# An fp32 two-stage linear layer on TensorE: the sums of x blocks and of the folded weight move from VectorE to GpSimd

## What is computed

```
cond = einsum('bsi,oi->bso', x, weight) + bias                       # 2048 x 2048
     + scale[b] * einsum('bsr,bor->bso', einsum('bsi,bri->bsr', x, a_sel), b_sel)   # rank 16
w    = (NF4[codes].reshape(-1, 64) * absmax[:, None]).reshape(2048, 2048)
out  = x + einsum('bsd,od->bso', cond, w) + bias2
```

## Time and profile before

| what | us |
|---|---|
| median of 3 runs | 2275.09 (2272.87 to 2276.41) |
| the profiled execution | 2272.21 |
| its span | 2270.1 |
| PE busy | 2189.5 (96%) |
| DVE busy | 1862.0 (82%) |
| ACT busy | 1114.2 (49%) |
| POOL busy | 0.2 |

### The profile page before, as it was taken

One profiled execution on the slowest core, in us unless ns is written; L12 is line 12 of the kernel. 1 busy time (PEld: TensorE's weight loads), 2 busy tenths in 40 slices (PEclk: granted clock), 3 DMA queues, 4 the chain that ended last, 5 costly groups with the idle time before them and its releaser, 6 DMA issues.

```text
span 2270.1 us, 32172 instructions
## 1 busy us (share of the span) xinstructions
PE 2189.5 (96%) x12194; PEld 1870.2 (82%) x12194; DVE 1862.0 (82%) x2795; ACT 1114.2 (49%) x1494; POOL 0.2 (0%) x4
## 2 busy tenths in 40 slices
PE   3589999999999999999999999999999999999999
PEld 2468877887888777889999988888988888988888
DVE  8989988987898565488887789888798888898887
ACT  7766666664666333344444444334444343443432
POOL 0000000000000000000000000000000000000000
PEclk8699999999999999999999999999999999999999
DMA  8477877887787798877777877777887777977775
GB/s 191 139 235 241 253 238 240 253 263 233 248 256 252 251 300 274 259 241 236 245 237 234 278 263 252 239 243 250 281 273 240 242 244 248 302 254 239 242 249 172
DMA packets 403535, 558.02 MB, mean 246 GB/s; under 512 B 42008, under 2 KB 256664, under 8 KB 403256
## 3 DMA queue, kind: packets, MB, share of 16 engines
q1 hardware_dynamic: 403384, 555.98, 77.4%
HBM read 427.96 MB, written 128.99 MB: 245 GB/s over the span
## 4 chain that ended last, share of the span: by engine, by line
PE 93%; DVE 5%; ACT 1%; DMA 1%; issue 0%; DVEq 0%; SPq 0%; ACTq 0%
PE ps L1332 26%; PE ps L1171 14%; PE ps L1173 14%; PE ps L1172 14%; PE ps L1333 13%; PE ps L1336 4%; PE ps L1182 2%; PE ps L1335 2%; PE ps L1215 1%; PE ps L1166 1%; DVE wq_nat L839 0%; DVE wq_nat L842 0%; DVE deq_e L858 0%; DVE deq_e L855 0%; DVE wq_nat L864 0%
## 5 line engine op out<-in xcount | busy, mean ns | idle before, releaser
L1332 PE MATMUL ps<-comb,xs 128*128 128x512 f32 x2527 | 903.3, 395 | 0.8 <-DVE comb L936 0.8
L679 ACT CAST xs<-xr 128x1024 fp32r<-128x1024 f32 x427 | 448.2, 1051 | 625.5 <-DMA xr<-xc_d 625.2
L1333 PE MATMUL ps<-comb,xs 128*128 128x256 f32 x2527 | 707.8, 280 | 0.0
L942 DVE TENSOR_TENSOR xs<-xr,xs 128x1024 fp32r<-128x1024 f32 x427 | 521.3, 1221 | 128.8 <-ACT xs L679 126.1
L1332 PEld LDWEIGHTS ps<-comb,xs 128*128 128x128 f32 x2527 | 474.3, 188 | 103.4 <-DVE comb L936 1.1
L1333 PEld LDWEIGHTS ps<-comb,xs 128*128 128x128 f32 x2527 | 475.4, 188 | 14.5
L1171 PE MATMUL ps<-wq,tile 128*128 128x512 f32 x1088 | 468.8, 431 | 0.0
L1173 PE MATMUL ps<-wq,tile 128*128 128x512 f32 x1088 | 427.9, 393 | 0.0
L1172 PE MATMUL ps<-wq,tile 128*128 128x512 f32 x1088 | 427.1, 393 | 0.0
L1171 PEld LDWEIGHTS ps<-wq,tile 128*128 128x128 f32 x1088 | 205.7, 189 | 66.0 <-issue 2.8
L1173 PEld LDWEIGHTS ps<-wq,tile 128*128 128x128 f32 x1088 | 205.6, 189 | 45.3
(11 more groups left out here) (115 smaller groups left out, 2401.0 us busy)
## 6 DMA issues: line engine op xcount, KB each, us to landing
xr<-xc_d SPq DMA_DIRECT2D x427, 512.0 KB, 3.9
raw<-in_L_cond_weight_dram SPq DMA_DIRECT2D x128, 512.0 KB, 4.3
xc_d<-rq SPq DMA_DIRECT2D x26, 1792.0 KB, 7.3
x_nat<-in_x_dram SPq DMA_DIRECT2D x128, 256.0 KB, 3.8
res<-in_x_dram SPq DMA_DIRECT2D x64, 512.0 KB, 5.3
out_dram<-res SPq DMA_DIRECT2D x128, 256.0 KB, 4.4
wc_d<-cs SPq DMA_DIRECT2D x32, 896.0 KB, 4.6
comb_raw<-wc_d SPq DMA_DIRECT2D x28, 1024.0 KB, 7.8
```

What stands on the lines that cost most here:

```text
L679: nc.scalar.copy(xs[f][:, HI, :, :], xr[f][:, LO, :, :]).then_inc(s_xhi, 1)
L942: tt(xs[f][:, LO, :, :], xr[f][:, LO, :, :], xs[f][:, HI, :, :].bitcast(F32), ALU.subtract).then_inc(s_xlo, 1)
L1332: nc.tensor.matmul(bank[:, :], x_hi, both, start=(k == 0), stop=False)
L1333: nc.tensor.matmul(bank[:, 0:HW], x_lo, high, start=False, stop=False)
```

## The change

`weight_sums` and `x_sum` are taken out of DVE's program and put, with the same operands, semaphores and waits, into a new program on GpSimd that runs over the same jobs: in job g first `weight_sums`, then `x_sum` step 3 in odd jobs, and steps 0 to 2 in even ones. ACT's and SP's programs and their waits are as before.

```diff
@@ DVE
-            def weight_sums(j, k):
...
-            def x_sum(m, step):
...
             for g in range(JOBS):
...
-                if s % 2 and s >= 3:
-                    weight_sums(j, (s - 3) // 2)
-                if s == 0 and j:
-                    weight_sums(j - 1, HK - 1)
                 if n is not None:
                     dequantise_a(n)
-                if g % 2 and 3 <= g <= 2 * UNITS + 1:
-                    x_sum((g - 3) // 2, 3)
                 if n is not None:
                     dequantise_b(n)
-                if g % 2 == 0 and 2 <= g <= 2 * UNITS:
-                    x_sum(m, 0)
...
-                if g % 2 == 0 and 2 <= g <= 2 * UNITS:
-                    x_sum(m, 1)
-                    x_sum(m, 2)
...
-            weight_sums(NS - 1, HK - 1)
@@ GpSimd
+        @block.gpsimd
+        def _(pool):
+            tt = nc.gpsimd.tensor_tensor
+
+            def weight_sums(j, k):
+                g, t0 = S1 * j + 2 * k + 2, 4 * (HK * j + k)
+                pool.wait_ge(s_evac, evacs(g))
+                if k == 0:
+                    pool.wait_ge(s_gst, 16 * (j + 1))
+                    pool.wait_ge(s_btst, 16 * min(j + 1, NS - 1))
+                b11, b21, t2, t1, b12, b22, t4n = (cs[:, f, :] for f in range(NF))
+                tt(t1, b12, b11, ALU.subtract).then_inc(s_tcomb, 1)
+                tt(b12, b22, b12, ALU.subtract).then_inc(s_tcomb, 1)
+                pool.wait_ge(s_tcomb, t0 + 1)
+                tt(t2, b22, t1, ALU.subtract).then_inc(s_tcomb, 1)
+                pool.wait_ge(s_tcomb, t0 + 3)
+                tt(t4n, b21, t2, ALU.subtract).then_inc(s_tcomb, 1)
+
+            def x_sum(m, step):
...
+            for g in range(JOBS):
+                j, s = divmod(g, S1)
+                if s % 2 and s >= 3:
+                    weight_sums(j, (s - 3) // 2)
+                if s == 0 and j:
+                    weight_sums(j - 1, HK - 1)
+                if g % 2 and 3 <= g <= 2 * UNITS + 1:
+                    x_sum((g - 3) // 2, 3)
+                if g % 2 == 0 and 2 <= g <= 2 * UNITS:
+                    for step in range(3):
+                        x_sum((g - 2) // 2, step)
+            weight_sums(NS - 1, HK - 1)
```

More of the change, by code:

```diff
@@ L1080, in _ @@
                 j, s = divmod(g, S1)
-                n, m = pieces_of(g), (g - 2) // 2
+                n = pieces_of(g)
                 if s == 1:
@@ L1157, in _ @@
             add_lora(2 * ALL_PAIRS - 1, PRODUCTS - 1)
+        @block.gpsimd
[15 more added lines that the diff above has]
+            def x_sum(m, step):
+                a11, a12, s2, s1, a21, s4, a22 = (rq[:, f, :, :] for f in range(NF))
+                if m < EARLY:
+                    pool.wait_ge(s_back, 32 * (m + 1))
+                if step == 0:
+                    pool.wait_ge(s_xcp, 4 * m + 2)
+                    ins = tt(s1, a21, a22, ALU.add)
+                elif step == 1:
+                    pool.wait_ge(s_xcp, 4 * m + 3)
+                    ins = tt(a21, a11, a21, ALU.subtract)
+                elif step == 2:
+                    pool.wait_ge(s_sums, 4 * m + 1)
+                    ins = tt(s2, s1, a11, ALU.subtract)
+                else:
+                    pool.wait_ge(s_xcp, 4 * m + 4)
+                    pool.wait_ge(s_sums, 4 * m + 3)
+                    ins = tt(s4, a12, s2, ALU.subtract)
+                ins.then_inc(s_sums, 1)
+            for g in range(JOBS):
[10 more added lines that the diff above has]
+            weight_sums(NS - 1, HK - 1)
         @block.tensor
```

## The result

The changed kernel took 2289.86 us in the median of 4 runs (2288.18 to 2291.45); the kernel before, run beside it, 2274.26 us in 4 runs (2272.87 to 2276.41). The ratio is 1.007, with a 95% interval of 1.0058 to 1.0082: **15.6 us slower**, within the range and with the sign of the forecast, which had said 23 us. Three executions among all that follow, one of E8 and two of the kernel before beside it, ran far slower (3136 to 10897 us) and are left out of every figure.

The account below looks back on a forecast made before the run. PE bounds the kernel, with DVE hidden behind it. DVE held up by GpSimd adds costs +16 us in the first slice and +6 in the next two, together +23 (rounded up): 2298 us, own range 2280 to 2320, overall 2272 to 2335.

Parts of the forecast that it names:

- its relief: DVE's lighter load: saves PE's wait of about 0.13 us at first-slice job edges, 1 us, taken as nothing.
- GpSimd's price: Eight adds a pair on GpSimd: 1.14 us for 128x512 and 0.60 for 128x256, 6.9 us a pair.
- a DVE instruction with two SBUF operands stands still: Such DVE instructions wait while a two-SBUF-operand GpSimd add runs: 5.9 us blocked a pair.
- the others: L836, L845 and L877 on DVE, taken as not held up by GpSimd adds: 2.94 of 19.08 us a pair.
- the high share: Part of GpSimd's add time assumed to block DVE: 85% of 6.9 us, 5.9 us a pair.
- 8 pairs: Number of job pairs in the first slice, each taken to grow by 2.03 us.
- The +16: First slice's forecast loss: DVE's 24.98 us a pair against PE's 22.95, +16 us.
- The second slice: DVE's 25.08 us a pair against PE's 24.68, +0.40 us a pair, 3 us longer.
- The third slice: Same pattern as the slice before it: blocked DVE exceeds PE by 0.40 us a pair, 3 us longer.
- rival C: Third slice: late x-sum store delays ACT's copy into rq; +10 us on top of the forecast, 2308 us; chance 0.07.
- At nothing I cost these: SP's stores and queued tile loads, GpSimd's code preparation and the turn to the products: taken to cost 0 us.
- The fourth slice and the products: After 774 us: DVE, busy 54% in the slice, can be held up for nothing; both unchanged.

Follow-up runs that it names:

- E8: Changed kernel with the first slice's sums back on DVE, and x_sum step 3 and its store ahead of weight sums in odd jobs throughout: 2284.32 us.
- E1: Changed kernel with one GpSimd memset in place of each sum, same waits, nothing read: 2273.58 us.
- E7: Changed kernel with a GpSimd copy of one operand in place of each sum, same waits: 2272.57 us.
- E10: Changed kernel with fill, one-column fill, fill in place of each sum, lasting about as long as an unhindered add: 2276.44 us.
- E12: Kernel before, all sums on DVE, plus 40 GpSimd adds in jobs 3 to 12 into a buffer nobody reads: 2297.29 us.
- E2: Changed kernel with three successive GpSimd fills in place of each sum, about as late as the hindered adds, nothing read: 2291.73 us.
- E3: Changed kernel with only the x sums on GpSimd, the weight sums left on DVE: 2291.29 us.
- E4: Changed kernel with only the weight sums on GpSimd, the x sums left on DVE: 2281.55 us.
- E6: Changed kernel with x_sum step 3 and its store ahead of the weight sums and theirs in odd jobs: 2286.94 us.

## Why the prediction was right

**DVE's slack was none, and its relief was worth nothing.** Right: 0.8 us in E1, E7 and E10, against the 1 us given.

**GpSimd's price.** Forecast 1.14 and 0.60 us, measured 1.28 and 0.73, unhindered; 8.1 us a pair, not 6.9, and 10.5 as they ran. The nearest row of before was a fair guide, but each add takes some 0.14 us more. The estimate from the Trainium skill (GPSIMD Engine Reference, section 3.1), a quarter and an eighth of its figure for 2048 elements, 1.12 and 0.56 us, was low by a little more; the trace shows the 1.28 and 0.73. I hadn't thought of the adds being held up themselves, and that stretch turned out to matter.

**Who is held up.** The step "a DVE instruction with two SBUF operands stands still" is shown by E12 and by the 167 meetings above. That L877 is spared is right (683 ns). That L836 and L845 are spared is wrong: 545 and 589 ns for 420 and 421. The sentence of the Trainium skill cited there (SBUF — State Buffer, section "Who interferes with whom") speaks of two SBUF inputs, and the trace agrees for those, down to the waiting for the end of the instruction under way. The prediction took only that half of the section: it also lets a `tensor_scalar` contend when it runs in a mode that uses both ports. No run shows the mode as such, but the two TENSOR_SCALARs are held up as it says, beside adds and, in E2, beside fills. So these two didn't belong to "the others", and a larger share than 85% of DVE's work could meet an add.

**How much.** This was the choice on which the sum hung, and it was too high: 5.9 us a pair (85% of 6.9), measured 5.0, 5.3 and 4.4. As a share of the adds' bare length that is 62%, 65% and 54%. Two errors partly cancel, the low price and the high share. The runs show one limit that the share left out. With large adds alone (E3) a meeting costs a two-operand instruction 1.03 us in the median of 105, with small ones alone (E4) 0.35 us in 73, less than the adds' own 1.28 and 0.73. Four of each are 5.5 us a pair, 68% of 8.1, an estimate from these of what is lost if every add is met once. With the measured 5.16 us the working of the first slice gives 19.08 + 5.16 = 24.24 against 22.95, 1.3 us a pair. The "8 pairs" are the other step that was mis-sized. In the kernel before, PE's pair lasts 22.95 us only up to the fifth, and 24.67 from the sixth on, when PE transposes x as well; DVE's 24.24 fits into that. The slice lost 8.5 us, 8.4 of them at its first six edges. The +16 came from the same step with 2.03 us and eight pairs.

**The second slice.** Forecast +3, measured +0.2. The margin of 5.50 us a pair was right; 5.3 us fits into it, 5.9 doesn't. E3 shows how narrow such a reading by pairs is: there it says nothing is lost, and 5.5 us are.

**The third slice.** The size was forecast at +3, for the wrong reason. The hold-up of 4.4 us fits into the 5.50 there. The 5.3 us are rival C's for the most part: E6 gives back 3.7 of them by moving one sum and its store, and E10 has 3.4 of them with no add on GpSimd at all. I had priced C at 10 us on top and given it 0.07. It should have stood in the sum, since its row showed no slack at all. Its working kept the 7.3 us to landing, and it is that term too which moved, to 8.6 us, with the two stores issued closer together. That the third slice came out near its +3 is luck.

**"At nothing I cost these", SP's queue.** Wrong as a rule, though not by what the forecast came to. E2 and E8 each lose 8 to 12 us in the first slice through what stands behind late or bunched stores, with no DVE instruction of two operands held up. The path that does it, store of x sums, load of the next early blocks into the same `rq`, sums, has no term in the prediction. In the change itself it takes 24.3 us a pair, as DVE does, but PE waits for DVE alone. E10 says that the path is that long because the adds are stretched; so in the first slice both go back to DVE and GpSimd in each other's way. What would be left if only DVE's hold-up were mended in the change was not tried; with only the path given room, in E6, the first slice loses 10.4 us.

**The fourth slice and the products** were unchanged, 0.0 and +0.9 us, as the forecast had them.

So the sign was right, and so was the mechanism for the first slice, which has 8.5 of the 15 us. Its size there was given double, 16 us, by 5.9 for 5 us a pair and by eight pairs for six edges; the third slice's loss came from a late store that had no place in the sum. The errors partly cancel, and the sum came out 7 us too high.

## What to carry to other kernels

Before work is moved off an engine, look whether PE waits for that engine at all; here it waited 1.5 us in 826, so all that the move could do was to add costs. Adds with two SBUF operands on GpSimd do not run beside VectorE's instructions of that kind but in turn with them: 54 to 65% of their bare length came back as longer VectorE instructions in the first three slices, and a VectorE at 90% has no room for it. And follow each moved result to the store that frees its buffer, to what is loaded into that buffer next, and to what SP has queued behind it: a buffer with one copy and no slack costs as much as a slow engine, and by job, not by pair.

## What the hardware showed that I had not expected

- The hindrance goes both ways, and by whole instructions. In the trace of the change each of 167 DVE instructions that started inside an add (with over 0.2 us of it left) ended 0.13 to 0.20 us before the add's end plus its own length; of 152 adds that started inside such a DVE instruction, 151 did the same the other way round, 0.12 to 0.14 us before. A GpSimd add of 128x512 takes 1.28 us alone and 1.5 to 1.8 in the mean beside DVE; one of 128x256 takes 0.73 and 0.95 to 1.06.
- So it comes in steps. In the pair shown a DVE instruction of 0.69 us takes 1.04 to 1.12 or 1.60 to 1.67, one of 0.42 takes 0.93 to 0.96.
- A GpSimd copy, with one operand, holds DVE up for as long as it lasts, just as an add does (63 of 63 in E7).
- Writes of GpSimd alone (fills) leave two-operand DVE instructions at 692 ns, in 163 of 163 meetings in E2, but not the two TENSOR_SCALARs: one took up to 1194 ns for 418 there, the other up to 847 for 421.
- A store of the x blocks took 7.4, 8.6 and 9.9 us to land in the median of the third slice (kernel before, change, E10), issued 2.9, 1.7 and 1.2 us behind the store of weight sums.
- At the fastest a GpSimd fill of 128x512 took 0.52 us, a copy 0.61 and an add 1.28; in the mean they took 0.53 (E1), 0.89 (E7) and 1.68 (the change).
